# Last scores and last up-projections in banks of their own, seven outputs made beside the last feed-forward, centred values copied out

## The reference

```
x = x + tanh(g_xattn) * cross_attention(layernorm(x), ctx)
y = layernorm(x)
for i in range(6):
    y = attention_i(shift_tokens(y)) + y    # 16 heads of 64, windows of 32 that see 64 keys, l2norm, rotary
    y = ffn_i(shift_tokens(y)) + y          # layernorm, up to 2 x 341, a * gelu(gate), down to 128
out = x + tanh(g_ffn) * y
```

## Time and profile before

| | us |
|---|---|
| median of 3 runs | 1982.19 (1978.48 to 1985.48) |
| the profiled execution | 1982.28 |
| its span in the profile | 1980.5 |
| PE busy | 1858.9 (94%) |
| DVE busy | 1584.1 (80%) |
| ACT busy | 1046.7 (53%) |
| POOL busy | 904.7 (46%) |

### The profile page before, as it was taken

The page is one execution under the profiler, slowest core; times in us unless marked ns, Lnnn a source line. Parts: engine busy times, 40 slices in busy tenths (PEclk is TensorE's granted clock), DMA queues, the critical chain, the costliest instruction groups (busy, mean ns, idle before and its releaser), DMA issues.

```text
span 1980.5 us, 84861 instructions
## 1 busy us (share of the span) xinstructions
PE 1858.9 (94%) x35408; PEld 1299.7 (66%) x35408; DVE 1584.1 (80%) x3084; ACT 1046.7 (53%) x1879; POOL 904.7 (46%) x1231
## 2 busy tenths in 40 slices
PE   6888868899999999999999999999999999999996
PEld 3445435667667676777677676777777676767674
DVE  4566547888888888888888888888888898888883
ACT  2444433565645555565655555564555555565653
POOL 1000024464645555564646555464646455464640
PEclk9899888999999999999999999999999999999997
DMA  2001025464666646565655666465665656664650
GB/s 69 10 8 64 0 32 93 72 95 81 104 113 97 105 72 108 102 105 93 92 91 88 112 108 107 74 95 111 101 103 81 101 74 122 109 94 81 92 91 22
DMA packets 73332, 166.87 MB, mean 84 GB/s; under 512 B 16592, under 2 KB 23504, under 8 KB 72400
## 3 DMA queue, kind: packets, MB, share of 16 engines
q0 software_dynamic: 36864, 100.71, 37.9%
q1 hardware_dynamic: 36432, 65.68, 12.9%
HBM read 20.57 MB, written 1.05 MB: 11 GB/s over the span
## 4 chain that ended last, share of the span: by engine, by line
PE 76%; DVE 11%; issue 8%; DMA 3%; ACT 1%; POOL 0%; DVEq 0%; SPq 0%; ACTq 0%; POOLq 0%
PE ps L1024 14%; PE ps L1060 8%; PE ps L1114 7%; PE ps L1134 6%; PE ps L1084 6%; PE ps L1168 5%; PE ps L1036 5%; PE ps L1097 4%; PE ps L1127 3%; PE ps L957 3%; DVE big L826 3%; PE ps L1158 3%; PE ps L1048 3%; DMA big<-big 3%; PE ps L937 2%
## 5 line engine op out<-in xcount | busy, mean ns | idle before, releaser
L476 POOL DMA_DIRECT2D big<-big x768 | 607.4, 1494 | 69.5 <-DVE big L818 51.0
L580 ACT ACTIVATE big<-ps 128x512 f32<-128x512 f32 x384 | 228.6, 595 | 571.9 <-PE ps L1024 523.7
L1024 PE MATMUL ps<-big,wn_sb 128*128 128x256 f32 x1536 | 409.9, 395 | 3.3 <-DVE big L818 3.2
L826 DVE TENSOR_TENSOR big<-big,ps 128x512 f32<-128x512 f32 x384 | 249.5, 680 | 94.1 <-PE ps L1048 84.3
L1024 PEld LDWEIGHTS ps<-big,wn_sb 128*128 128x128 f32 x1536 | 274.2, 191 | 55.9 <-DVE big L818 13.9
L467 POOL TENSOR_TENSOR big<-big 128x512 f32<-128x512 f32 x96 | 123.5, 1287 | 357.1 <-ACT big L597 357.1
L815 DVE TENSOR_TENSOR big<-ps,tab 128x512 f32<-128x512 f32 x384 | 262.1, 683 | 13.6 <-ACT big L580 13.5
L818 DVE TENSOR_TENSOR big<-ps,tab 128x512 f32<-128x512 f32 x384 | 259.2, 675 | 0.0
L1168 PE MATMUL ps<-big,wo_sb 128*128 128x256 f32 x768 | 214.8, 383 | 0.0
L442 POOL COPY big<-xs 64x256 f32 x144 | 79.7, 553 | 263.0 <-DVE xs L854 257.0
L1060 PE MATMUL ps<-wn_sb,big 128*64 128x512 f32 x768 | 183.3, 615 | 3.5 <-DVE big L818 3.5
(11 more groups left out here) (144 smaller groups left out, 2913.1 us busy)
## 6 DMA issues: line engine op xcount, KB each, us to landing
big<-big POOLq DMA_DIRECT2D x768, 128.0 KB, 4.9
big<-big SPq DMA_DIRECT2D x96, 256.0 KB, 4.2
big<-big SPq DMA_DIRECT2D x96, 192.0 KB, 4.5
wn_sb<-in_wn SPq DMA_DIRECT2D x6, 1024.0 KB, 9.7
wn_sb<-in_wn SPq DMA_DIRECT2D x6, 512.0 KB, 6.7
wo_sb<-in_wo SPq DMA_DIRECT2D x6, 512.0 KB
w_sb<-in_w SPq DMA_DIRECT2D x6, 341.0 KB, 3.0
w_sb<-in_w SPq DMA_DIRECT2D x6, 192.0 KB, 3.1
```

The costliest lines, as they stand in the source:

```text
L476: eng.dma_start(rot[to:to + 32, at:at + 4, :], src[32 * r:32 * r + 32], accum_op=ALU.add).then_inc(added[i], 16)
L580: eng.activation(sq[:, two, :], ps[:, i % 2, :].rearrange("p (a t) -> p a t", a=2), ACT.Square).then_inc(sq_d, 1)
L826: eng.tensor_tensor(hat[:, two, :], rot[:, two, :], ps[:, i % 2, :].rearrange("p (a t) -> p a t", a=2), ALU.mult).then_inc(hat_d, 1)
L1024: mm = eng.matmul(ps[:, k % 2, a * T:a * T + T], wn_sb[:, u * P:u * P + P], sT, start=True, stop=True)
```

## The change

It makes four edits.

1. The late layer norm: ACT copies the centred values from bank 0 to SBUF (`xc0`), and `norm_rows` reads that copy. `center` of chunks 1 and 2 then waits only for the copy; `variance` of chunks 1 and 2 gets a wait for `norm_rows` of the chunk before, which reads bank 1. The scratch tiles have two slots in place of three. In step 8 the matmuls of chunks 1 and 2 stand earlier in PE's order. `norm_rows` of chunk 3 moves from behind `n0` to behind `N6`.
2. Pass 48: the second chunk of scores goes to banks 0 and 1, does not wait for D1, and W0 waits for D0 and D1 alone.
3. Pass 49: F5 and F6 on PE go to banks 2 and 4 and wait neither for the gelus nor for DVE.
4. Outputs 0 to 6 move into pass 49: on DVE behind f3, on ACT behind the last gelu, on PE between F6 and F7. The table load behind that gelu is left out.

```
-        sq0, z0, z1 = (view(3 * CW, 3, CW) for _ in range(3))
+        sq0, z0, z1, xc0 = (view(2 * CW, 2, CW) for _ in range(4))
+        def up_bank(s, A, Bh):
+            return {4: 3, 5: 2, 6: 4}[s] if not A and not Bh else 3
+        def score_bank(c, r, A):
+            return r if c == 1 and not A else 5 + r
...  ACT, norm_squares
+                if c >= 2:
+                    eng.wait_ge(nxn, c - 1)
+                eng.activation(xc0[:, c % 2, :], ps[:, LN_BANKS[c][0], :], ACT.Copy).then_inc(nxc, 1)
...  ACT, body, behind the gelu of F5
-                        eng.preload_act_table_set("natural_log_exp_and_others")
+                        if A or Bh:
+                            eng.preload_act_table_set("natural_log_exp_and_others")
+                        else:
+                            outputs(0, B - 1)
...  DVE, norm_rows and body
-                eng.tensor_tensor(xs[:, 2 * c:2 * c + 2, 1:T + 1], ps[:, LN_BANKS[c][0], :]...
+                eng.tensor_tensor(xs[:, 2 * c:2 * c + 2, 1:T + 1], xc0[:, c % 2, :]...
+                        if not Bh:                  # behind N6, no longer behind n0
+                            norm_rows(CH - 1)
+                        if i == 3 and not A and not Bh:   # behind f3
+                            outputs(0, B - 1)
...  PE, center and variance
-                    eng.wait_ge(nxn, c)
+                    eng.wait_ge(nxc, c)
+                if 0 < c < CH - 1:
+                    eng.wait_ge(nt, 3 * c - 1)
...  PE, step 8
+                if late:
+                    center(1)                       # ahead of scores(4)
-                        for at, do, c in ((0, center, 1), (2, variance, 1), (4, center, 2), (6, variance, 2)):
+                        for at, do, c in ((0, variance, 1), (2, center, 2), (4, variance, 2)):
...  PE, score and weigh
-                        eng.wait_ge(sub_d, it * 4 + (2 - 4))
+                        if A:
+                            eng.wait_ge(sub_d, it * 4 + (2 - 4))
-                        eng.wait_ge(sub_d, it * 4)
+                        eng.wait_ge(sub_d, it * 4 - 2 * (not A))
...  PE, ffn
+                    alone = not A and not Bh
                     if s == 5:
-                        eng.wait_ge(fg, it * 3 - 4)
+                        if not alone:
+                            eng.wait_ge(fg, it * 3 - 4)
                     if s == 6:
-                        eng.wait_ge(fu, it * 3 - 5)
+                        if not alone:
+                            eng.wait_ge(fu, it * 3 - 5)
                         up("a", 0, 0)
                         up("a", 1, T).then_inc(fh, 1)
+                        if alone:
+                            outputs(0, B - 1)
```

More of the change, by code:

```diff
@@ L240, in gated_flamingo @@
         LN_BANKS = [(0, 1), (0, 1), (0, 1), (4, 5)]
-        nmean, nsq, nvar, nln, ny, nxn, nt = (
-            sem(n) for n in ("nmean", "nsq", "nvar", "nln", "ny", "nxn", "nt"))
+        nmean, nsq, nxc, nvar, nln, ny, nxn, nt = (
+            sem(n) for n in ("nmean", "nsq", "nxc", "nvar", "nln", "ny", "nxn", "nt"))
         fsh, fmean, fsq, fvar, fln, fy, fchain, fxc, fxn = (
@@ L488, in norm_squares @@
                 eng.wait_ge(nmean, c + 1)
-                eng.activation(sq0[:, c % 3, :], ps[:, LN_BANKS[c][0], :], ACT.Square).then_inc(nsq, 1)
+                eng.activation(sq0[:, c % 2, :], ps[:, LN_BANKS[c][0], :], ACT.Square).then_inc(nsq, 1)
+                if c >= 2:
+                    eng.wait_ge(nxn, c - 1)
+                eng.activation(xc0[:, c % 2, :], ps[:, LN_BANKS[c][0], :], ACT.Copy).then_inc(nxc, 1)
             def norm_roots(c):
                 eng.wait_ge(nvar, c + 1)
-                eng.activation(z0[:, c % 3, :], ps[:, LN_BANKS[c][1], :], ACT.Ln, bias=part["eps"]).then_inc(nln, 1)
+                eng.activation(z0[:, c % 2, :], ps[:, LN_BANKS[c][1], :], ACT.Ln, bias=part["eps"]).then_inc(nln, 1)
                 eng.wait_ge(nln, c + 1)
-                eng.activation(z0[:, c % 3, :], z0[:, c % 3, :], ACT.Exp, scale=-0.5).then_inc(ny, 1)
+                eng.activation(z0[:, c % 2, :], z0[:, c % 2, :], ACT.Exp, scale=-0.5).then_inc(ny, 1)
             def cross_body(b, X1, X2, X3):
@@ L571, in _, with outputs @@
             norm_roots(CH - 1)
+            def outputs(first, last):
+                for b in range(first, last):
+                    eng.wait_ge(tr_o, b + 1)
+                    eng.activation(otok[:, b, :, :], ps[:, b % 2, 0:T].rearrange("p (n d) -> p n d", n=NT),
+                                   ACT.Copy).then_inc(ev_o, 1)
             def body(b, it, l, A, Bh, F, first):
@@ L622, in body @@
                         eng.wait_ge(fh, it * 3 - 4)
-                        eng.activation(gt[0:m, 2, :], ps[0:m, 3, 0:T], ACT.Gelu, bias=vf[0:m, 11:12]).then_inc(fg, 1)
-                        eng.preload_act_table_set("natural_log_exp_and_others")
[L626 to L630, removed]
+                        eng.activation(gt[0:m, 2, :], ps[0:m, up_bank(5, A, Bh), 0:T], ACT.Gelu, bias=vf[0:m, 11:12]).then_inc(fg, 1)
+                        if A or Bh:
+                            eng.preload_act_table_set("natural_log_exp_and_others")
+                        else:
+                            outputs(0, B - 1)
             pipeline(eng, body, outputs=outputs)
@@ L741, in layer_second, with outputs @@
                 eng.tensor_copy(vf[:, :], src).then_inc(fvc, 1)
+            def outputs(first, last):
+                eng.wait_ge(fx, L * B - B + last + FREE)
+                for b in range(first, last):
+                    eng.scalar_tensor_tensor(x1[:, b, :], xs[:, b, 1:T + 1], gates[:, 1:2], x1[:, b, :], ALU.mult,
+                                             ALU.add).then_inc(gx, 1)
             def body(b, it, l, A, Bh, F, first):
@@ L801, in body @@
                         eng.tensor_scalar(n_s, ps[:, 2, 0:T], 1e-24, 65536.0, ALU.max, ALU.mult).then_inc(ss_d, 1)
-                        if not Bh:
-                            norm_rows(CH - 1)
                     if kind == "N":
@@ L854, in body @@
                         eng.tensor_tensor(xb, xb, ps[:, 2:3, T:2 * T], ALU.add).then_inc(x_d, 1)
[L856 to L860, removed]
             pipeline(eng, body, layer_start, layer_second, outputs)
@@ L878, in variance @@
                 eng.wait_ge(nsq, c + 1)
-                eng.matmul(ps[:, LN_BANKS[c][1], :], mean_w, sq0[:, c % 3, :], start=True, stop=True).then_inc(nvar, 1)
+                if 0 < c < CH - 1:
+                    eng.wait_ge(nt, 3 * c - 1)
+                eng.matmul(ps[:, LN_BANKS[c][1], :], mean_w, sq0[:, c % 2, :], start=True, stop=True).then_inc(nvar, 1)
             def cross_body(b, X1, X2, X3):
@@ L1011, in _, with outputs @@
             eng.wait_ge(nxn, CH - 1)
+            def outputs(first, last):
+                for b in range(first, last):
+                    eng.wait_ge(gx, b + 1)
+                    if b >= 2:
+                        eng.wait_ge(ev_o, b - 1)
+                    for n in range(NT):
+                        mm = eng.transpose(ps[:, b % 2, n * P:n * P + P], x1[:, b, n * P:n * P + P], ident)
+                    mm.then_inc(tr_o, 1)
             def body(it, A, Bh, F):
@@ L1074, in score @@
                             rows = slice(64 * r, 64 * r + 64)
-                            eng.matmul(ps[WIN * w:WIN * w + WIN, 5 + r, :], id32[rows, :],
+                            eng.matmul(ps[WIN * w:WIN * w + WIN, score_bank(c, r, A), :], id32[rows, :],
                                        mask_cb[rows, min(w, 1):min(w, 1) + 1, :].to_broadcast((64, 4, P)), start=True, stop=False,
@@ L1130, in ffn, with up @@
                 def ffn(s):
-                    def up(col, j, at, stop=True):
+                    alone = not A and not Bh
+                    def up(col, j, at):
                         o, m = HC[j]
                         o += HID * (col == "gate")
-                        return eng.matmul(ps[0:m, 3, at:at + T], w1_sb[:, o:o + m], xn, start=True, stop=True)
+                        return eng.matmul(ps[0:m, up_bank(s, A, Bh), at:at + T], w1_sb[:, o:o + m], xn, start=True, stop=True)
                     if s == 1:
@@ L1175, in body @@
                     steps[kind](i)
[L1177 to L1184, removed]
             passes(eng, body, outputs)
```

23 lines of the change are left out of this document (10 added, 13 removed).

## The result

| | before | after |
|---|---|---|
| median of 16 runs each | 1985.26 us (1976.11 to 2006.26) | 1971.14 us (1962.68 to 1981.98) |
| profiled execution, span | 1980.5 | 1968.0 |

The ratio of the two is 0.9934, 95% interval 0.992 to 0.9948: some 13 us less. The prediction was 1970.3, a gain of 12.0, counted from 1982.28. The time agrees with it; whether its parts do is another question.

What follows compares the result with a forecast made beforehand. PE bounds the 46 loop passes, so gains come only where it waits on serial ACT and DVE operations outside them. 3.9 + 1.6 + 0.6 + 5.9 = 12.0 us off 1982.28 gives 1970.3, range 1965.5 to 1977.5.

Steps and rivals of the forecast that it cites:

- Where the change can act: Only step 8 of the cross-attention, pass 0, and passes 48 and 49; the PE-bound loop passes stay at 34.00 us.
- Edit 1a: Step 8 of the cross-attention: center(2) waits only for chunk 1's copy; 19.69 us becomes 15.8, gain 3.9 (bounds 0.4 to 6.8).
- PE is at its lower level until about 263: Step 8 before the change: center(2) takes 2.04 us against 1.06 and the weigh behind it 3.57 against 1.86.
- Edit 1b: Pass 0: norm_rows(3) behind N6, so H0 starts at 300.6, not 302.21; gain 1.6 us (bounds 0 to 4.2).
- What is late next: Pass 0: the 2.85 us of norm_rows(3) itself; H0 held by POOL's adds stood only as the lower bound, 0.
- Edit 2: Pass 48: S1 some 2 us earlier, but D3, behind f0, only 0.6; gain 0.6 us (bounds 0 to 1.8).
- the pause inside W3: Pass 48: PE stands 1.44 us in the middle of W3, no semaphore behind it; forecast to stay there.
- Edits 3 and 4: Pass 49: 3.7 (F1 sooner) + 0.4 (to F7) + 1.8 (clock) = 5.9 us gain, bounds 3.3 to 6.5.
- (a): PE's clock stays low in pass 49 (gain 3.3) and falls in step 8 (gain 2.2): 1974.6 us; chance 0.16.
- (b): Pass 49: F7 held behind 14 transposes at the lower level, 8.3 us; 1977.1 us, no difference; chance 0.06.
- (c): Step 8 bound by ACT, pass 0 by the adds: 0.4 + 0 + 0.6 + 4, 1977.3 us; chance 0.09.
- (d): Loop no longer stays in PE's instruction store, a 2.06 us stall every pass: 95 us, 2065 in all; chance 0.03.

Runs made afterwards that it cites:

- the three later kernels that keep edit 2: Changed kernel with norm_rows of chunk 3 in the gaps of pass 0; that with early outputs; that with fillers too: ratios 0.9944, 0.9921, 0.9917.
- edit 4 alone: The changed kernel without edits 2 and 3, so edit 1 is in it too: ratio 0.996, 25.02 us from the residual to the end.
- the later one: The changed kernel timed and profiled once more, without an edit, against the kernel before: ratio 0.9955 (0.9927 to 0.9983).
- the fillers: Four matmuls with unread results added behind the transposes of the kernel with outputs in the idle time ahead of xn: median 1965.79 us, ratio 0.9917.
- edit 1b alone: The kernel before with only norm_rows of chunk 3 moved behind N6: ratio 0.9994, 14.52 us from n0 to the first row maximum.
- `norm_rows(3)` in the gaps: Changed kernel with norm_rows of chunk 3 spread over pass 0: two operations ahead of c0, one ahead of c2, one ahead of c4; ratio 0.9944.

## Why the prediction was right, point by point

- **Where the change can act.** Right: the loop passes away from layer changes are 34.00 before and 33.99 to 34.00 after, but for one of 34.44 before. The stretch from n0 of pass 3 to n0 of pass 47 scatters between 1504.3 and 1508.6 over all kernels, with or without edits.
- **Edit 1a, 3.9 forecast.** In the first pair it gave 3.3, and the sequence came nearly as summed, 0.6 longer: scores(3) and (4), split by center(1), take 0.9 more than together, not 0.6, and the waits are 1.3 ahead of variance(2) and 1.2 ahead of weigh(3). The step that failed is what it was compared with: "PE is at its lower level until about 263" was taken as a property of the old order. Undisturbed, the old order takes 26.70 and the new one 26.2 to 26.4: 0.4 from the order itself. What else it gives depends on whether the clock falls around the end of center(2)'s wait. It did in three of the five old profiles (29.75, 29.75, 35.80) and at that place in none of the seven new ones; in one old and one new it was low from before the step as well (35.80, 33.64), which the edit cannot help. The means, 29.7 and 27.3, differ by 2.4, on five and seven draws.
- **Edit 1b, 1.6 forecast.** 1.3 in the mean (16.06 to 14.74), so the term was nearly right, though not by its working: counted from `n0`, H0 came 0.4 later than forecast, behind two operations slowed from 0.69 to 1.02 and 1.09 beside POOL's copies, and PE then stood at the lower level through the H steps; against that, the old place is usually worse than in the profile I read. What is late next is first DVE and then, with DVE cleared, POOL's adds, which I had priced as a bound only.
- **Edit 2, 0.6 forecast.** D3 starts 23.04 behind n0 of pass 47 in all six old profiles and 22.38 to 22.58 behind it in the six new ones: 0.5 to 0.7 earlier, which bears the term out up to there, and f0 in front of D3 is in the chain. For the whole stretch the means are 42.98 and 42.26, 0.7, but the old column mixes levels of the clock. Where the stretch's mean granted clock is 0.96, the old code takes 43.46, 43.55 and 43.83 and the new one 41.83 to 42.61 in all six, 1.35 less in the mean; the two old ones at 1.00 (41.51, 41.20) are shorter than any new one, and the one at 0.92 is the 44.34 of the prediction. That the pause inside W3 would stay was half right: it stays (1.0 to 1.5, in the old code 1.1 to 1.8), and a second one can appear inside S1 (in both profiles of the changed kernel and in the one of edit 2 alone, in none of the three later kernels that keep edit 2), where it takes back part of what the missing wait gives. The cause of these pauses was not settled; no wait of the program is behind them.
- **Edits 3 and 4, 5.9 forecast.** 5.8 and 6.0. The working is borne out by its parts in the first pair: 3.5 up to the first up-projection (forecast 3.7), 0.4 from there to F7 (0.4), 1.9 from F7 to the end (1.8), with outputs in 3.35 (3.3) and F1 at once. Edit 3 alone gives 4.2, edit 4 alone 0.8, together 1 more than their sum, since the outputs cost 3.3 at the upper level and 4.1 at the lower, and only edit 3 brings the upper one back.
- **Rivals.** (a) did not come: not in pass 49, in any of three profiles, nor as a fall behind the waits of step 8; (b) is refuted by the pace of the outputs; (c) has a true half, the adds in pass 0; (d) did not come: no pause repeats in the loop. But its reading of the earlier trace rows was short: the trace of the kernel before has pauses at 319.03, 350.34 and 367.56 besides the one at 343.92.
- **The sum.** Stage by stage, 2.4 + 1.3 + 0.7 + 5.8 is 10.2 rather than 12.0. The timing of 16 runs each gave some 13 us, its interval 10.3 to 15.9, which 10.2 just misses; the later one gave some 9 (3.4 to 14.5). A term is lacking that the prediction put at nothing: from n0 of pass 1 to n0 of pass 3, where no step was moved, the five profiles with the old PE code ahead of the loop take 71.7 to 74.1 and the seven with the new one 69.0 to 71.5, 2.4 less in the mean, and what is gone there is pauses without a releaser (those of over 0.6 us come to 4.7 to 7.1 with the old code and to 2.2 to 4.7 with the new). With it the sum is 12.6. So the 12.0 was met partly by luck: step 8 was put 1.5 too high, and the pauses, which nobody had forecast, gave more than that back. Why they change with the code was not settled.

The best kernel seen is the one with the outputs in the idle time ahead of xn: 0.9921 (0.9897 to 0.9945) against before, and 0.9917 with the fillers, which is no different. Its advantage over the changed kernel rests on its stage (15.35 against 20.05 and 19.85), for the intervals of the whole runs overlap.

## What to carry to other kernels

A stage that waits has several lengths, by how much of it TensorE spends at each level of its clock, and a single profile shows one draw of them: compare a stage over several profiles, unedited ones too, and read its mean granted clock beside its length, before crediting an edit with it. Look at the stages that the edit doesn't touch as well: here one of them changed. At the end of a program, where nothing follows to fill an engine, first put independent outputs into time in which the engines stand idle anyway, and give each step of a serial run a bank of its own so that TensorE goes through in one piece; the second halved here also what came after it. Moving an operation from one place of an engine's order to another moves its hold; look who is queued behind the new place and what other engine works beside it.

## What the runs showed of the hardware

- The clock's return comes on top of the waits: after up-projections in one piece of 5.4 to 5.5 us F7 took 1.31 (changed kernel, the outputs' transposes in between) and 1.58 (edit 3 alone), where it takes 2.94 behind the same work with three pauses of about 1 us. With edit 3 alone F7 also began 2.8 sooner (6.4 behind the first up-projection in place of 9.2), so of its 4.2 the shorter way is the larger part.
- With seven outputs' transposes between F2 and F4 the clock did not fall in PE's idle time before xn (2.05 us left idle); in the changed kernel PE stands idle there from 1949.96 to 1953.60, and F4 begins at the lower level, as it did before. No run tried lengths between these.
- VectorE's 128x512 operations with both operands in SBUF took 1.02 and 1.09 in place of 0.69 while GpSimd ran its copies (an addition of zeros, L446) beside them, and the pair of copies 1.76 in place of 1.43. Two other runs part the causes. With edit 1b alone the last of the four operations still reads its centred values from PSUM and keeps 0.69 beside the copies, while the one ahead of it takes 1.01. With `norm_rows(3)` in the gaps, where no copy runs beside it, the last operation has both operands in SBUF and takes 0.68, and the copies take 1.43. The Trainium skill ("GPSIMD Engine Reference", "Specifications") has it that the two engines share SBUF interfaces and get in each other's way where a VectorE instruction has two SBUF inputs; the rows agree. Edit 1b alone:

```profile
301.32 1.76 POOL L441 TENSOR_TENSOR big<-xs,zeros 64x256 f32<-64x256 f32 x2
301.49 1.01 DVE L647 SCALAR_TENSOR_TENSOR big<-big 128x512 f32<-128x512 f32 x1
302.53 0.69 DVE L649 TENSOR_TENSOR xs<-ps,big 128x512 f32<-128x512 f32 x1
```

`norm_rows(3)` in the gaps:

```profile
282.84 0.68 DVE L664 TENSOR_TENSOR xs<-big 128x512 f32<-128x512 f32 x1
...
295.75 1.43 POOL L446 TENSOR_TENSOR big<-xs,zeros 64x256 f32<-64x256 f32 x2
```
